# Second condition's softmax reciprocals moved one chunk later in the projection, and four weight tiles of the MLP asked for ahead of its gate and bias rows

## The reference, cut to what matters

```
ada = silu(c) @ W_ada + b_ada          # shift, scale, gate for attention and for the MLP
h = layernorm(x) * (1 + scale_msa) + shift_msa
q, k, v = h @ W_qkv + b_qkv
o = softmax(q k^T / sqrt(36)) v
x = x + gate_msa * (o @ W_proj + b_proj)
h = layernorm(x) * (1 + scale_mlp) + shift_mlp
x = x + gate_mlp * (gelu(h @ W_fc1 + b_fc1) @ W_fc2 + b_fc2)
```

## Time and profile before

| | |
|---|---|
| runs, median | 3441.5 us |
| profiled execution | 3447.29 us |
| its span | 3445.6 us |
| TensorE busy | 3407.4 us, 99% |
| VectorE, ScalarE, GpSimd busy | 1975.8, 1493.9, 369.1 us |
| TensorE clock granted, mean | 0.997 |

### The profile page before, as it was taken

How to read it: one execution, slowest core, us unless ns; L and a number is a source line. 1 busy time by engine, 2 the same in 40 slices (tenths; PEclk the granted TensorE clock), 3 DMA queues, 4 the chain that set the end, 5 groups by cost and what they waited for, 6 DMA issues and landing times. The chain is left out here.

```text
span 3445.6 us, 46544 instructions
## 1 busy us (share of the span) xinstructions
PE 3407.4 (99%) x16991; PEld 2283.2 (66%) x16991; DVE 1975.8 (57%) x3574; ACT 1493.9 (43%) x2801; POOL 369.1 (11%) x289
## 2 busy tenths in 40 slices
PE   7999999999999999999999999999999999999999
PEld 5888855455454545445454554547988989898988
DVE  5446566767676766777667676754543333433332
ACT  3223255556555555555555555565531111211110
POOL 1000010111100000001000000015610101000000
PEclk9999999999999999999999999999999999999999
DMA  6554431211212111121211112114751212421211
GB/s 207 178 163 147 132 98 29 60 46 41 57 30 55 30 50 34 32 54 34 54 30 50 35 32 53 30 39 151 264 171 43 86 44 85 134 79 50 73 57 52
DMA packets 133110, 265.89 MB, mean 77 GB/s; under 512 B 18628, under 2 KB 39876, under 8 KB 125972
## 3 DMA queue, kind: packets, MB, share of 16 engines
q1 hardware_dynamic: 132888, 262.91, 25.5%
HBM read 164.51 MB, written 97.26 MB: 76 GB/s over the span
## 5 line engine op out<-in xcount | busy, mean ns | idle before, releaser
L1209 DVE TENSOR_REDUCE q_mx<-b_sp 128x1 f32<-128x512 f32 x1968 | 1196.0, 675 | 228.2 <-PE b_sp L1147 228.2
L1266 ACT ACTIVATE b_pt<-b_st 128x512 f32<-128x512 f32 x2009 | 1013.3, 627 | 441.0 <-PE b_st L1164 433.8
L1177 PE MATMUL b_op<-b_pt,b_vs 128*37 128x512 f32 x4096 | 929.4, 596 | 0.0
L1177 PEld LDWEIGHTS b_op<-b_pt,b_vs 128*37 128x37 f32 x4096 | 223.9, 113 | 567.1 <-issue 440.2
L2053 ACT ACTIVATE d_af<-n_pf,q_mx 128x512 f32<-128x512 f32 x140 | 96.2, 687 | 699.6 <-PE n_pf L1952 697.7
L1970 PE MATMUL d_pm<-d_vh,d_ah 128*128 128x288 f32 x1152 | 340.4, 296 | 1.6 <-DVE d_al L2005 1.6
L1971 PE MATMUL d_pm<-d_vl,d_ah 128*128 128x288 f32 x1152 | 340.5, 296 | 0.0
L1972 PE MATMUL d_pm<-d_vh,d_al 128*128 128x288 f32 x1152 | 340.3, 295 | 0.0
L1332 POOL TENSOR_TENSOR w_oc<-b_oa,b_ob 37x512 f32<-37x512 f32 x127 | 163.1, 1284 | 1590.1 <-DVE b_ob L1242 1584.0
L1147 PE MATMUL b_sp<-q_hh,q_lo 108*128 108x512 f32 x688 | 283.9, 413 | 0.9 <-PEq L951 0.9
L1164 PE MATMUL b_st<-q_qs,q_ks 110*128 110x512 f32 x697 | 275.9, 397 | 0.9 <-ACT b_pt L1266 0.9
(11 more groups left out here) (344 smaller groups left out, 4763.2 us busy)
## 6 DMA issues: line engine op xcount, KB each, us to landing
qkh<-a_th SPq DMA_DIRECT2D x72, 256.0 KB, 2.0
qkl<-a_tl SPq DMA_DIRECT2D x72, 256.0 KB, 2.1
d_yi<-y SPq DMA_DIRECT2D x64, 288.0 KB, 3.0
n_oi<-hw SPq DMA_DIRECT2D x12, 1024.0 KB, 5.8
vd<-a_vx SPq DMA_DIRECT2D x8, 1184.0 KB, 6.8
b_vs<-vd SPq DMA_DIRECT2D x32, 296.0 KB, 2.8
a_x<-in_x SPq DMA_DIRECT2D x8, 1152.0 KB, 7.1
ot<-w_oc SPq DMA_DIRECT2D x128, 72.0 KB
```

The lines of the kernel that those rows point to most:

```text
L1177: ins = e.matmul(op[64 * a:64 * a + VW, :], vs[h % 2][:, 2 * j + a, :], pt[g % NP][:, a * 512:a * 512 + 512], start=j == 0, stop=j == 7)
L1209: e.tensor_reduce(mx[:, k // 4, k % 4:k % 4 + 1], sp[slot % 4][:, :], AX.X, ALU.max).then_inc(s_mx, 1)
L1266: e.activation(pt[g % NP][:, a * 512:a * 512 + 512], bank(x)[:, :], ACT.Exp, scale=SCALE).then_inc(s_p, 1)
```

## The change

The reciprocals for the second condition are taken behind VectorE's addition of (1, 5) where they were taken behind that of (0, 4); their high part is made at (1, 7) where it was at (0, 6), and their rest behind the addition of (2, 0) where it was behind that of (1, 0). The placing, which was split (chunks 4, 5 and 6 at step (1, 5), chunk 7 at (2, 5)), is done for all four chunks at (2, 5). So the first turn of chunk 4 now waits for all eight transfers, where it waited for six. In the MLP tiles 19 to 22 of W_fc2 are asked for ahead of the gate and bias rows, and tile 23 behind them.

```diff
@@ phase_proj, sync
-            elif kind == "project" and (c, n) == (HCH - 3, 5):
-                e.wait_ge(s_ta, KT * (HCH - 1))
-                for n in range(HCH - 1):
+            elif kind == "project" and (c, n) == (HCH - 2, 5):
+                e.wait_ge(s_ta, KT * HCH)
+                for n in range(HCH):
                     W.place(e, 1, n)
-            elif kind == "project" and (c, n) == (HCH - 2, 5):
-                e.wait_ge(W.s_rr, 32 * (2 * HCH - 1))
-                e.wait_ge(s_ta, KT * HCH)
-                W.place(e, 1, HCH - 1)
@@ phase_proj, tensor
-                    e.wait_ge(W.s_rr, 32 * (HCH if c < HCH else 2 * HCH - (c < NCH - 1)))
+                    e.wait_ge(W.s_rr, 32 * (HCH if c < HCH else 2 * HCH))
@@ phase_proj, vector
-                if m == 4:
+                if (c, n) == (1, 5):
                     W.invert(e, 1)
-                elif m == 8:
+                elif (c, n) == (2, 0):
                     W.low(e, 1)
@@ phase_proj, scalar
-                if (c, n) == (0, 6):
+                if (c, n) == (1, 7):
                     W.high(e, 1)
@@ phase_mlp, sync
-        for k in range(W2[0], W2[0] + 4):
+        for k in range(W2[0], W2[0] + 8):
             load_w(k)
...
-        for k in range(W2[0] + 4, W1[1]):
+        for k in range(W2[0] + 8, W1[1]):
             load_w(k)
```

## The result

The changed kernel took 3447.6 us (median of 14 executions, 3444.4 to 3450.1), the kernel before beside it 3442.6 (14 executions). The ratio is 1.0015, with a 95% interval of 1.0008 to 1.0022: 5.2 us slower, between 2.8 and 7.6. The forecast was 0.4 us faster, range 3435.5 to 3445.5.

What follows compares the result with a forecast made beforehand. TensorE, busy 99% of the span, was taken as the bound, with at best 7.7 us to win. The projection's +0.6 and the MLP's -1.0 gave -0.4 us on 3441.5, so 3441.1 us, range 3435.5 to 3445.5.

Steps and rivals of the forecast that it cites:

- MLP, -1.0: MLP's first pass: tile 19 lands earlier and the gelu wait goes; 1.0 us gained (0.1 to 1.3).
- with 5.15 us or more like tile 19 before: MLP: tile 23, issued behind the rows at about 2535.5, takes this long to land; its copy stays about 2541.10.
- The head start: Projection, chunk 0: without the reciprocals the wait ahead of chunk 1 and its slow clock go, 3.5 us earlier.
- 2.7 us shrinking: Projection: the head start falls to 2.7 us at chunk 0's normalised tiles, with a wait there of some 1.5 us.
- the branch that I took: Projection, chunk 1: GpSimd is done with its bias, so the reciprocals' rest costs 0.6 us net; 1.0 us gain left.
- What swallows it: Projection, 2400 to 2420 us: full DMA engines keep `c_x` of chunk 3 in line; chunk 2's tiles gain only 0.3 us.
- 0 to 0.5 us; I take 0.3: Projection: what `c_x` of chunk 3 gains because six small transfers left the line ahead of it.
- The rival of that name: "The head start lives": `c_x` lands 2 us or more earlier, up to 2.7 us reach the end; 3437.8 to 3436.3, chance 0.2.
- The new wait, +0.6: Projection, chunk 4's first turn: eight transfers land at 2418.7, 1.3 us late; 0.73 is taken up, leaving 0.6 late.
- My second rival: Chunk 4's first turn: TensorE comes 1.0 us early, stands 2.3 us, clock falls; +2.1 us, 3443.5, chance 0.25.
- The sum: Whole kernel: 0.6 - 1.0 = -0.4 us on the median of 3441.5, giving 3441.1 us.

Runs made afterwards that it cites:

- run 1: Kernel before with the MLP's edit alone (tiles 19 to 22 ahead of the rows): 3445.0 us against 3442.2 before, ratio 1.0007.
- run 4: Changed kernel with the two stores of hidden tiles issued behind fc2's first results: 3449.8 us against 3442.2 before, ratio 1.0022.
- run 7: Kernel before with the MLP's edit, the four loads reading 128 different rows of W_fc2 (output not the block's): 3444.4 us against 3442.5 before, ratio 1.0004.
- run 3: Changed kernel with tile 23 too ahead of the rows, so all nine tiles: 3443.0 us against 3442.2 before, ratio 1.0003.
- run 5: Kernel before with all nine tiles ahead of the rows, projection untouched: 3440.3 us against 3442.5 before, ratio 0.9992.
- run 6: Changed kernel with nine tiles ahead of the rows and three of four placings ahead of chunk 3's load of x: 3444.0 us against 3442.5 before.
- run 9: Kernel before with reciprocals in VectorE's gap at chunk 0's end and nine tiles ahead of the rows: 3437.5 us against 3442.4 before, ratio 0.9987.
- run 11: Kernel before with nine tiles ahead of the rows, projection untouched, measured a second time: 3438.9 us against 3442.4 before, ratio 0.9989.
- run 13: Kernel before with reciprocals in VectorE's gap, nine tiles ahead, GpSimd's products held until the first pass's last hidden rest: 3437.5 us against 3443.1 before.
- run 8: Kernel before with only the placing moved, all four pairs at (2, 5): 3446.1 us against 3442.5 before, ratio 1.0007.
- run 2: Kernel before with the projection's edits alone (reciprocals and placing): 3445.0 us against 3442.2 before, ratio 1.0009.
- run 12: Kernel before with reciprocals in VectorE's gap and all four pairs placed at (2, 5): 3444.6 us against 3443.1 before, ratio 1.0004.
- run 10: Kernel before with reciprocals in VectorE's gap at chunk 0's end, MLP untouched: 3439.5 us against 3442.4 before, ratio 0.9993.

## Why the prediction was wrong

**MLP, -1.0: the step that failed.** Its parts held: tile 19 landed in 2.7 us (forecast 3.7), the wait for the gelu went, tile 23 was issued 11.4 us after the phase's start (2535.5 - 2524.0 = 11.5). The term that failed is "with 5.15 us or more like tile 19 before", which the sum took as a landing near 2541.10, 17.1 us after the phase's start. It landed after 8.2 us, at 19.6. The 5.15 us were those of a tile issued 3.2 us after the first row (2526.89 in the trace of before), when 3.2 of the 7.6 us in which the rows were served had passed; it landed 8.3 us after the issue of the first row. Tile 23 is issued 1.9 us after the first row, at the heels of the last, and pays for nearly all of them. Counted from the first row, 8.3 us give a landing at 17.8, which is 0.7 of the 2.5 us by which I was wrong. The other 1.8 are that the five loads took longer as a group: 10.1 us from the first issue to the tile's landing, 10.5 in run 1, 9.6 in run 4. Run 7's 1.9 us are no answer to these 1.8, since the rows of before were read 128 times too. Nor is it the number of loads: with the tile ahead of the rows (runs 3, 5, 6, 9, 11 and 13) the same five take 8.1 to 8.4 us from the first issue to the last landing. Up to 0.5 us may be the stores behind (run 4); the rest stays open. The Trainium skill (DMA: Bandwidth & Descriptors, Queues, rings and completion order) has descriptors taken in ring order; the tile's landing 0.7 us behind the last row agrees. I had weighed that rule against the placing and not against this edit. Behind the late tile everything in two engines' lists came late, GpSimd's products fell on its rest (0.8 us, which I had as a bound). Against the profile of before TensorE waits 1.9 us more in this phase, and the low clock behind it lasts about twice as long (3.4 us lost against 1.6). Measured: +2.8 us for this edit alone.

**The head start.** Right in its working. No wait ahead of chunk 1, full clock, 2.7 us shrinking: chunk 0's transposes waited 1.67 us, the reciprocals began at 2387.93 and ended in front of `q_lo` at 2391.19, with the rest 0.67 us long since GpSimd was done, the branch that I took. The addition of (2, 0) came 40.35 us after the phase's start (forecast 2398.8 - 2358.45 = 40.35). Wrong in its base: 1.5 of the 3.5 us were the low clock behind the wait ahead of chunk 1, which I took for a property of the kernel. In runs 1, 5, 7, 8 and 11, with the same wait (1.7 to 2.0 us), the clock held. Run 11 has the very same wait:

```profile
2373.06 0.37 PE L1597 MATMUL n_pf<-e_wh,c_ah 128*128 128x288 f32 x1 [2.02 <-issue]
...
2373.00:2377.00 4.00, 3.94 (x29) 3.93 (x30) 2.26 (x5) 0.44 (x1) 2.91 (x3) 1.00 0.58 204
```

So most executions had only some 2 us to win there.

**What swallows it.** Right against the one profile: `c_x` landed 58.8 us after the start, against 58.9 before. Against the four others of the old code (58.0 to 58.1) it is later, and in runs 2 to 4 too (59.1 to 59.4). The term "0 to 0.5 us; I take 0.3" for the small transfers that left the line had the wrong sign: with all eight behind it `c_x` lands 1.0 us later, 57.1 in run 12 against 56.1 in run 10, and 59.0 in run 8 against 58.0 to 58.1. Why, stays open. And I took the full engines for the reason that nothing is gained. But in all fifteen profiles `c_x` lands 19.8 to 21.1 us after the store of y behind (1, 7) is issued, even in run 6, where the load itself went out 3.8 us later than in the changed kernel. So this store sets the place in the line: with the reciprocals in the gap (run 10) it goes out 2.5 us sooner than before, `c_x` lands at 56.1, and the whole head start lives. The rival of that name was real, at the price of another place for the reciprocals than the change gave them.

**The new wait, +0.6: the second step that failed.** The landing was right (60.4 us after the start, forecast 2418.7 - 2358.45 = 60.25), and so was what it takes up: the wait of 0.73 us ahead of chunk 2's transposes is gone. But the sum set it against a TensorE that comes to the turn where it came before, at 2417.34, 58.9 us after the start. It came 0.9 us earlier, at 58.0, as it also does in the four other profiles of the old code (58.0 to 58.4), in which the clock hadn't fallen. So it stood 2.1 to 2.7 us in the five profiles with the change's placing and reciprocals in chunk 1 or the gap, and 2.3 in run 8. My second rival had this, with 2.3 us and the low clock, at +2.1; the wrong choice was to let it rest on one threshold. In the six profiles with this wait the clock held in two (2.38, 2.26 us) and fell in four (2.10, 2.12, 2.27, 2.68). The two edits of the projection cost 2.9 us in run 2, the placing alone 3.7 in run 8.

**The sum.** 2.8 + 2.9 = 5.7 us, against 5.2 measured for both. Rightly foreseen was that no more than 0.2% would be at stake; wrongly, the sign of the MLP's term and the size of the projection's. The measured time lies 2.1 us above my range.

## What to carry to other kernels

Before moving a transfer behind others, add up from the profile when those are served, counted from the issue of the first; the time to landing of a transfer that was issued later is too short for one issued at once. Work moved off one engine's critical stretch should go where that engine is idle in the trace, and not merely later: the same 3.33 us cost nothing in a gap of 3.85 us, and cost the head start ahead of a store that opens a line of transfers. Where a wait near 2 us changes place, price it with the low clock behind it, since executions differ. And take a low clock in one profile for the luck of that execution until a second shows it: 1.5 us of my forecast's base was in no other profile of the same code.

## What was not expected of the hardware

- Four loads of 288 KB that read one row 128 times, and one tile behind them, were served in 10.5 us from the first issue (run 1); with 128 different rows each in 8.6 (run 7: 2530.21 to 2532.11 + 6.7). With the tile first and the rows behind it the five took 8.1 to 8.4 (runs 3, 5, 6, 9, 11 and 13).
- Whether the clock falls behind a wait did not follow its length: it held after a wait of 3.44 us for normalised tiles in run 5 and fell after 2.10 in run 12; ahead of chunk 1 it fell after 2.02 in the profile of before and held after 2.02 in run 11. In the MLP of the kernel before it fell behind waits of 0.73, 0.43 and 0.43 us, and in run 8 the same three left it at 1.00.
- A CAST of VectorE on a 128x512 tile, with one input, takes 0.42 us and beside GpSimd's product 1.63 (runs 9 and 13). Which of two instructions suffers seemed to hang on which began first: VectorE's took 1.81 us when it began 0.14 us behind GpSimd's (run 5), 1.86 when 0.10 behind (run 6), and 0.69 when it began 0.02 or 0.03 us ahead (runs 3 and 11). I had looked for the slowing only in instructions with two inputs. The Trainium skill (SBUF — State Buffer, Who interferes with whom) names `cast` among what can contend with GpSimd; these rows agree.
- An issue of 32 KB, mostly 0.6 us, held SyncE for 1.33 us while the DMA engines were full (run 6).
